# One-hot buffers handed over in two halves, x W1 inside the edge counting, and degrees from a column of ones, in a four-layer graph network on one NeuronCore

## The chip, the cores and the metric

The kernel runs on one core of a Trainium2 chip. The metric is device time in microseconds (us) of one execution, 5030.59 in the median of three runs. The engines are TensorE (PE in the profile, its weight loads PEld), VectorE (DVE), ScalarE (ACT), GpSimd (POOL) and SyncE (SP), which issues the DMAs. Each runs its own instructions in order; they meet at semaphores.

## The reference, cut to what matters

A graph has 1250 nodes with 512 features, and 20000 edges `src -> dst`, sorted by `dst`, each with a weight. Four blocks follow each other, each with a residual and a layer norm. Only the first is touched:

```python
deg  = segment_sum(ones, dst, 1250) + 1.0
inv  = rsqrt(deg)
def gcn_conv(x, W, b):                     # twice, relu after each
    h   = x @ W
    agg = segment_sum(h[src] * (inv[src] * inv[dst])[:, None], dst, 1250)
    return agg + h * (inv * inv)[:, None] + b
h = relu(gcn_conv(relu(gcn_conv(x, W1, b1)), W2, b2))
h = gru(h, W_ih, W_hh, b_ih, b_hh)         # 1250 steps one after the other
x = layernorm(x + h @ W_fc + b_fc)
```

The other blocks are a two-sided convolution with batch norm, a mixture of four experts over mean aggregation, and an aggregation by the edge weights. They use the edge count matrix, 1 / max(degree, 1) and the edge weight matrix that the first part of the kernel makes.

## The kernel before, in words

Nodes are cut into NT = 10 tiles of NP = 125. `adj_v` is the 1250 x 1250 matrix of edge counts (source on partitions and tiles, destination on columns), `wt_v` that of summed weights. Aggregation is a matrix product with `adj_v`.

*Counting.* The 160 groups of EP = 125 edges form 80 pairs (halves h = 0, 1), and the destinations 25 windows of WD = 50 columns. For each window DVE goes over the pairs that touch it. For each half it builds two one-hot matrices: `src_hot` (125 edges x 1250 sources, padded to HOT = 1254; before.py line 879) and `dst_hot` (125 x 4 x 50, with a one and the three parts of the edge weight, line 880). There is one buffer for each half. PE (`window`, lines 396 to 414) multiplies them: for each of the ten source tiles three small matmuls (line 411), 30 for each half, summed in two PSUM banks. `hot_ready0/1` hands a buffer to PE, `hot_used0/1` gives it back after the 30 matmuls. Matmuls with a matrix of zeros open and close a window (lines 403 and 414), and ACT (`take_window`, line 685) copies it out, with two sets of banks in turn. PE, DVE and ACT loop over windows; PE reads two registers from `bounds` at each window's start, and DVE two with some arithmetic.

*Between counting and conv1.* SP writes the counts (line 218) and the weights (line 220) to DRAM. PE sums the count matrix over the sources with a matrix of ones, 30 matmuls (line 426), the in-degree in a row on all partitions. DVE adds one (line 893), takes the maximum with one (line 894); PE turns the degrees into columns (line 435); GpSimd takes the power -0.5 (line 301); PE spreads the root over all partitions (line 443) between tiles of h1 = x W1 (`rows_product`, line 353), which ACT copies to `hn` (line 668). DVE adds the self loops on the diagonal (line 909) once the counts are out, and scales `adj_v` by the root of source and destination (line 910).

*conv1 and after.* `agg_cols` (line 363) makes 12 column blocks of 417 by ten matmuls each in four banks; ACT adds the bias with relu (line 660) into `r2`. PE turns `adj_v` block by block (line 458), and DVE copies the turned matrix to `wt_v` (line 919), which SP writes to DRAM for a later block. h2 and conv2 go as h1 and conv1, beside DVE's work on the recurrent weights (lines 922 to 953). Then come the input products of the recurrent stage (line 476, read out on DVE at line 969) and its 1250 steps (line 495), from about 693 to 3896 us.

Of the kernel before, what the change touches and what calls it, by code (L numbers as in the profile page):

```python
# [26 lines left out]
ALU = mybir.AluOpType  # L27
# [7 lines left out]
P = 128  # L35
# [16 lines left out]
COPIES = 16  # L52


def layout(nc, io):

    ctx = ExitStack()
    with ctx:
# [62 lines left out]
        e_col = hn_f[:, 1250:1250 + 3 * ET].rearrange("p (a t) -> p a t", a=3)  # L121
        e_src, e_dst, e_w = e_col[:, 0], e_col[:, 1], e_col[:, 2]
        w_part = hn_f[:, 1730:2370].rearrange("p (t a) -> p t a", a=4)
# [10 lines left out]


# [66 lines left out]
        def _(sp):  # L202
# [48 lines left out]
            sp.wait_ge(s("cnt_out0"), 16)  # L251
# [32 lines left out]
        def _(pool):  # L284

            pool.memset(ident[:], 0.0).then_inc(s("ident0"), 1)
# [4 lines left out]
            pool.wait_ge(s("ident0"), 1)  # L291
# [45 lines left out]
        def _(pe):  # L337
# [39 lines left out]
            pe.wait_ge(s("const"), 9)  # L377
# [17 lines left out]
            pe.wait_ge(s("plan"), 4)  # L395
            def window(w, u):
# [23 lines left out]
            for w in range(NW // 2 * 2, NW):  # L420
# [7 lines left out]
            pe.wait_ge(s("xcols_in"), 16)  # L428
            pe.wait_ge(s("w1_in"), 16)

            pe.wait_ge(s("win_read"), NW + 2)

            pe.wait_ge(s("deg1"), 3)
            for t in range(NT):
                m = mm(psum[0:NP, 7, t:t + 1], inv_row[0:1, t * NP:(t + 1) * NP], ones[0:1, 0:1], start=True, stop=True, skip_group_check=True)
            m.then_inc(s("deg1_turn"), 1)

            def inv_everywhere(h1_tile):

                if h1_tile == 2:  # L440
                    pe.wait_ge(s("inv_col_ready"), 1)
                    for t in range(NT):
                        m = mm(psum[:, 4 + t // 4, (t % 4) * NP:(t % 4 + 1) * NP], inv_col[0:NP, t:t + 1].to_broadcast([NP, P]), ident[0:NP, 0:NP],
                               start=True, stop=True, skip_group_check=True)
# [839 lines left out]
```

## Time and profile before

| What | us |
|---|---|
| median of three runs | 5030.59 (5028.41 to 5030.91) |
| the profiled execution | 5028.03 |
| its span, first to last instruction | 5025.8 |
| TensorE busy | 4893.7 (97%) |
| TensorE weight loads busy | 4218.9 (84%) |
| DVE busy | 2881.4 (57%) |
| ACT busy | 1950.6 (39%) |
| mean granted TensorE clock, share of full speed | 0.988 |

The profile is one execution. Busy time is counted for each engine; matmuls are pipelined, so their busy times overlap and a mean is longer than the distance from one to the next. "Idle before" is the time in which the engine did nothing ahead of an instruction, with what ended it; "issue" there means that nothing in the profile ended it. fp32 matmuls stand as two records each. A merged row of the timeline gives the start of the first and the time to the end of the last of its instructions.

### The profile page before, as it was taken

Reading aid. Unit: us, or ns where it says so; the run is one execution under the profiler, and the core shown is the slowest. Engines: PE = TensorE matmul, PEld = TensorE weight load, DVE = VectorE, ACT = ScalarE, POOL = GpSimd, SP = SyncE. Lnnn points to the kernel's source line nnn. Section 1 sums busy time; section 2 is a strip of 40 time slices with the busy share of each in tenths; the row PEclk is TensorE's granted clock in tenths of the full one; section 3 lists DMA queues with packets and bytes.
Section 4 is the critical chain, followed back from the end, with each engine's and each line's share of the span. In section 5 each row is a group of like instructions: output and inputs, shape, how many; then the busy total and the mean of one; then the engine's idle time right before and its main releaser. Section 6 shows DMA issues by size and latency. Waiting matters only on the chain.

```text
span 5025.8 us, 335766 instructions
## 1 busy us (share of the span) xinstructions
PE 4893.7 (97%) x131794; PEld 4218.9 (84%) x131795; DVE 2881.4 (57%) x16350; ACT 1950.6 (39%) x15372; POOL 841.4 (17%) x5071
## 2 busy tenths in 40 slices
PE   7889999999999999999999999999999999999989
PEld 7765569999999999999999999999999445555554
DVE  6551346666666666666666666666666625445551
ACT  0110025555555555555555555555555001122110
POOL 0000002222222222222222222222222000000000
PEclk9999999999999999999999999999999999999989
DMA  1011210000000000000000000000000100011011
GB/s 62 0 67 67 99 49 0 0 0 0 0 0 0 0 0 0 0 0 0 0 0 0 0 0 0 0 0 0 0 0 0 60 17 20 18 36 37 25 50 41
DMA packets 28932, 81.11 MB, mean 16 GB/s; under 512 B 1594, under 2 KB 1834, under 8 KB 28858
## 3 DMA queue, kind: packets, MB, share of 16 engines
q1 hardware_dynamic: 28858, 80.03, 4.3%
q8 instruction: 57, 0.93, 0.1%
q14 instruction: 17, 0.14, 0.0%
HBM read 58.08 MB, written 21.95 MB: 16 GB/s over the span
## 4 chain that ended last, share of the span: by engine, by line
PE 94%; DVE 2%; issue 2%; DVEq 1%; ACT 0%; POOL 0%; DMA 0%; ACTq 0%; SPq 0%; POOLq 0%
PE psum L495 63%; PE psum L567 8%; PE psum L363 5%; PE psum L353 4%; PE psum L579 4%; PE psum L411 3%; PE psum L476 2%; PE psum L553 2%; PE psum L643 2%; DVE r L880 1%; PE psum L426 0%; PE psum L458 0%; DVEq L875 0%; DVE r L879 0%; DVE stat L813 0%
## 5 line engine op out<-in xcount | busy, mean ns | idle before, releaser
L495 PE MATMUL psum<-h,r 128*128 128x16 f16 (+1 forms) x80000 | 3008.5, 181 | 9.6 <-ACT psum L707 4.5
L495 PEld LDWEIGHTS psum<-h,r 128*128 128x128 f16 x80000 | 2639.5, 96 | 11.0 <-DVEq L993 5.2
L495 PE MATMUL psum<-h,hn 128*128 128x16 f16 (+1 forms) x40000 | 2124.3, 177 | 0.0
L495 PEld LDWEIGHTS psum<-h,hn 128*128 128x128 f16 x40000 | 1591.5, 96 | 0.0
L999 DVE TENSOR_TENSOR_SCAN psum<-mul_rz,psum 128x6 f32<-128x6 f32 x5000 | 854.3, 171 | 536.7 <-PE psum L495 488.1
L707 ACT COPY psum<-big 128x2 f32 (+1 forms) x7506 | 1003.3, 163 | 0.0
L315 POOL TENSOR_TENSOR upd_add<-upd,signs 128x4 f32<-128x4 f32 x2500 | 499.3, 200 | 2542.0 <-DVE upd L1018 1779.2
L720 ACT ACTIVATE mul_n<-psum 128x2 f32<-128x2 f32 x2500 | 433.7, 173 | 1123.2 <-DVE psum L999 1123.1
L1018 DVE TENSOR_TENSOR_SCAN upd<-upd_mul,upd_add 128x8 f32<-128x8 f32 x2500 | 418.1, 167 | 300.4 <-ACT upd_mul L725 300.4
L729 ACT ACTIVATE upd_add<-psum 128x2 f32<-128x2 f32 x2500 | 433.1, 173 | 297.5 <-DVE psum L1005 297.5
L1014 DVE TENSOR_TENSOR_SCAN h<-upd_mul,upd_add 128x8 f16<-128x8 f32 x2500 | 425.8, 170 | 169.2 <-POOL upd_add L315 4.4
L1028 DVE TENSOR_TENSOR h<-upd,h 128x2 f16<-128x2 f32 x2500 | 421.7, 169 | 86.1
L316 POOL COPY r<-upd 128x2 f32 x2500 | 468.5, 187 | 0.0
L1005 DVE TENSOR_TENSOR_SCAN psum<-mul_n,psum 128x8 f32<-128x8 f32 x2500 | 446.6, 179 | 33.6
L725 ACT ACTIVATE upd_mul<-psum 128x2 f32<-128x2 f32 x2500 | 433.2, 173 | 49.5
L411 PE MATMUL psum<-r 125*128 125x50 bf16 (+1 forms) x6240 | 240.2, 197 | 15.4 <-DVE r L880 11.2
L363 PE MATMUL psum<-adj,hn 125*128 125x417 f32 (+1 forms) x720 | 252.7, 512 | 2.1 <-ACT hn L668 1.4
L411 PEld LDWEIGHTS psum<-r 125*128 125x128 bf16 x6240 | 226.5, 100 | 28.6 <-DVE r L880 24.1
L363 PEld LDWEIGHTS psum<-adj,hn 125*128 125x128 f32 x720 | 135.7, 189 | 119.6 <-issue 115.0
L567 PE MATMUL psum<-adj,r 128*125 128x512 f16 x960 | 217.3, 383 | 8.3 <-DVE r L1210 8.3
L567 PEld LDWEIGHTS psum<-adj,r 128*125 128x125 f16 x960 | 132.0, 138 | 87.6 <-issue 13.1
L353 PE MATMUL psum<-ws,r 128*125 128x512 f32 x400 | 180.2, 613 | 7.2 <-ACT r L747 5.9
(224 smaller groups left out, 2532.7 us busy)
## 6 DMA issues: line engine op xcount, KB each, us to landing
ws<-in_Wl SPq DMA_DIRECT2D x9, 1024.0 KB, 5.4
ws<-in_Wr SPq DMA_DIRECT2D x9, 1024.0 KB, 7.6
edge_counts<-adj SPq DMA_DIRECT2D x2, 3051.8 KB
edge_weights<-big SPq DMA_DIRECT2D x1, 6103.5 KB
adj_rows<-big SPq DMA_DIRECT2D x1, 6103.5 KB
adj<-adj_rows SPq DMA_DIRECT2D x1, 6103.5 KB
big<-edge_counts SPq DMA_DIRECT2D x1, 6103.5 KB
adj<-edge_weights SPq DMA_DIRECT2D x1, 6103.5 KB
```

Of the source, the lines that this page charges most:

```text
L315: pool.tensor_tensor(start[:, :, 1:3], new[:, :, 2:3].broadcast_to([P, 2, 2]), signs[:].rearrange("p (j a) -> p j a", a=2), ALU.mult).then ...
L316: pool.tensor_copy(r1[:, 2 * c:2 * c + 2, bass.ds(t, 1)], upd[:, 1 - u, c, 2:8:4]).then_inc(s(f"gru_kept{c}"), 1)
L363: m = mm(o[:, 0:n1 - n0], rows[0:NP, t, f * P:(f + 1) * P], mat[0:NP, t, n0:n1], start=(t == 0), stop=(t == NT - 1))
L411: m = mm(to, src_hot[0:EP, h, t * NP:t * NP + P], dst_hot[0:EP, h, columns], start=False, stop=False, skip_group_check=True)
L495: m = mm(places, whh16[g][:, part, 2 * kc + k, (2 * c + j) * P:(2 * c + j + 1) * P], state.unsqueeze(1).broadcast_to([P, COPIES, 2 - part] ...
L567: m = mm(o, a(pa), b(pb), start=start and i == 0, stop=stop and i == 2)
L707: return nc.scalar.copy(columns, big[:, bass.ds(t * 12 + c * 6 + 2 * g, 2)])
L720: nc.scalar.activation(mul_n[:, c, 3:8:4], sum_rz[c][0][:, 2:6:3], ACT.Sigmoid).then_inc(s(f"gru_r{c}"), 1)
L725: nc.scalar.activation(upd_mul[:, c, 2:8:4], sum_rz[c][1][:, 2:6:3], ACT.Sigmoid).then_inc(s(f"gru_z{c}"), 1)
L729: nc.scalar.activation(upd_add[:, c, 0:8:4], sum_n[c][:, 3:8:4], ACT.Tanh).then_inc(s(f"gru_n{c}"), 1)
L999: v.tensor_tensor_scan(sum_rz[c][g], mul_rz[:], psum[:, 4 * c + g, 0:6], 0.0, ALU.mult, ALU.add).then_inc(s(f"gru_{'rz'[g]}_sum{c}"), 1)
L1005: v.tensor_tensor_scan(sum_n[c], mul_n[:, c], psum[:, 4 * c + 2, 0:8], 0.0, ALU.mult, ALU.add).then_inc(s(f"gru_n_sum{c}"), 1)
```

## The change

It has these parts:

- `src_hot` is built and given back in two parts of 625 columns: DVE builds columns 0 to 624 after `hot_part` (PE done with tiles 0 to 4), then `dst_hot` after `hot_used` (all ten), and signals `hot_first`; then columns 625 to 1249, and signals `hot_ready`. PE waits for `hot_first` ahead of tile 0 and for `hot_ready` ahead of tile 4, which reads up to column 627.
- A column of ones at 1250 of `src_hot` makes row 125 of the last tile of `adj_v` the in-degree. The 30 matmuls of line 426 go; ten turns of one column give degree columns, and everything else comes from these. Both 1/degree and the root are spread over the partitions by ten matmuls each, before conv1.
- h1 = x W1 is made inside the counting loop in bank 4: half a tile (two of four products) ahead of each of windows 0 to 23, the operand staged and the result copied by ACT. Twelve rounds for ten tiles; two tiles are made twice.
- The counts are written out in five transfers of 250 columns, as windows are done, in place of two at the end.
- `adj_v` is no longer scaled. The rows of h are scaled on ACT, the columns of the result on DVE (`scale_cols`), then ACT adds the bias with relu in place (`shift_cols`). The turned matrix is scaled on DVE as it is copied. The edge columns and weights move from `hn` to `big`, and the addition of the output bias to x moves behind counting's end.

The core of the diff, with `...` where lines are left out:

```diff
+H1 = NW // 2
...
+        x_stage = big[:, tail + 7 * ET:tail + 7 * ET + KT * NP].rearrange("p (k n) -> p k n", k=KT)
...
-            sp.wait_ge(s("win_counts"), NW)
-            for h in range(2):
-                half = slice(5 * h, 5 * h + 5)
-                sp.dma_start(tiles(d_cnt[half]), adj_v[0:NP, half]).then_inc(s(f"cnt_out{h}"), 16)
+            for q in range(NW // 5):
+                sp.wait_ge(s("win_counts"), 5 * q + 5)
+                columns = slice(5 * q * WD, (5 * q + 5) * WD)
+                sp.dma_start(tiles(d_cnt)[:, :, columns], adj_v[0:NP, :, columns]).then_inc(s(f"cnt_out{5 * q // (NW - 5)}"), 16)
...
+            pool.memset(src_hot[:, :, N:N + 1], 1.0).then_inc(s("const"), 1)
+            pool.memset(src_hot[:, :, N + 1:HOT], 0.0).then_inc(s("const"), 1)
...
-            def agg_cols(name, bank0, rows, mat):
+            def agg_cols(name, bank0, rows, mat, read="stored", first=None):
...
-                        o = out_rows(i, bank0, None, f"{name}_stored")
+                        o = out_rows(i, bank0, None, f"{name}_{read}")
                         for t in range(NT):
+                            if first and i == 0:
+                                first(t)
...
+            def h1_half(i, u):
+
+                if u == 0:
+                    pe.wait_ge(s("x_staged"), i + 1)
+                    pe.wait_ge(s("h1_stored"), i + 1)
+                for k in range(2 * u, 2 * u + 2):
+                    m = mm(psum[0:NP, 4], x_stage[:, k], wslot(0)[:, k], start=(k == 0), stop=(k == KT - 1), skip_group_check=True)
+                if u == 1:
+                    m.then_inc(s("h1_done"), 1)
...
                     for h in range(2):
-                        pe.wait_ge(s(f"hot_ready{h}"), g + 1)
                         for t in range(NT):
+                            if t == 0:
+                                pe.wait_ge(s(f"hot_first{h}"), g + 1)
+                            if t == 4:
+                                pe.wait_ge(s(f"hot_ready{h}"), g + 1)
...
+                            if t == 4:
+                                m.then_inc(s(f"hot_part{h}"), 1)
                         m.then_inc(s(f"hot_used{h}"), 1)
...
-            with pe.Fori(0, NW // 2) as i:
+            pe.wait_ge(s("w1_in"), 16)
+            with pe.Fori(0, H1) as i:
                 for u in range(2):
+                    h1_half(i, u)
                     window(2 * i + u, u)
...
             pe.wait_ge(s("win_counts"), NW)
-            for c, (n0, n1) in enumerate(NCH):
+            for t in range(NT):
+                m = mm(psum[0:NP, 7, t:t + 1], adj_v[:, NT - 1, t * NP:(t + 1) * NP], ident[:, NP:NP + 1], start=True, stop=True, skip_group_check=True)
+            m.then_inc(s("plan_turned"), 1)
+            pe.wait_ge(s("win_read"), NW + 2)
+            pe.wait_ge(s("h1_stored"), H1 + 1)
+            for b, (name, column) in enumerate((("invdeg_col_ready", invdeg_col), ("inv_col_ready", inv_col))):
+                pe.wait_ge(s(name), 1)
                 for t in range(NT):
-                    m = mm(psum[:, 4 + c, 0:n1 - n0], ones[0:NP], adj_v[0:NP, t, n0:n1], start=(t == 0), stop=(t == NT - 1))
-                m.then_inc(s("deg"), 1)
...
-            rows_product("h1", 0, r1, wslot(0), before=inv_everywhere)
-            pe.wait_ge(s("h1_stored"), NT)
-            pe.wait_ge(s("norm"), NT)
-            agg_cols("conv1", 4, hn, adj_v)
...
+            pe.wait_ge(s("invdeg_ready"), 1)
+            agg_cols("conv1", 4, hn, adj_v, "scaled", first=lambda t: (pe.wait_ge(s("h1_scaled"), t + 1), pe.wait_ge(s("loops"), t + 1)))
...
+            with act.Fori(0, H1) as i:
+                take_window(2 * i, 0)
+                act.wait_ge(s("h1_done"), i + 1)
+                nc.scalar.copy(hn[0:NP, bass.ds(i * NT // H1, 1)].rearrange("p t n -> p (t n)"), psum[0:NP, 4]).then_inc(s("h1_stored"), 1)
+                stage((i + 1) % H1)
+                take_window(2 * i + 1, 1)
...
+            for t in range(NT):
+                nc.scalar.activation(hn[0:NP, t], hn[0:NP, t], ACT.Copy, scale=inv_col[0:NP, t:t + 1]).then_inc(s("h1_scaled"), 1)
...
+                        dve.wait_ge(s(f"hot_part{h}"), offset + pair + 1)
+                        v.tensor_scalar(src_hot[0:EP, h, 0:N // 2], iota16[0:EP, 0:N // 2], e_src[0:EP, bass.ds(column, 1)], None, ALU.is_equal)
                         dve.wait_ge(s(f"hot_used{h}"), offset + pair + 1)
-                        v.tensor_scalar(src_hot[0:EP, h], iota16[0:EP], e_src[0:EP, bass.ds(column, 1)], None, ALU.is_equal)
...
-                            op0=ALU.is_equal, op1=ALU.mult).then_inc(s(f"hot_ready{h}"), 1)
...
+                            op0=ALU.is_equal, op1=ALU.mult).then_inc(s(f"hot_first{h}"), 1)
+                        v.tensor_scalar(src_hot[0:EP, h, N // 2:N], iota16[0:EP, N // 2:N], e_src[0:EP, bass.ds(column, 1)], None, ALU.is_equal).then_inc(s(f"hot_ready{h}"), 1)
...
+            def add_loops(t0, t1):
...
+            dve.wait_ge(s("cnt_out0"), 64)
+            add_loops(0, NT - 2)
+            for b, row_of in enumerate((invdeg_row, inv_row)):
+                dve.wait_ge(s("inv_rows"), b + 1)
+                for c in range(3):
+                    n0, n1 = 4 * NP * c, min(4 * NP * (c + 1), N)
+                    link(v.tensor_copy(row_of[:, n0:n1], psum[:, 4 - 4 * b + c, 0:n1 - n0]))
+                dve.sem_inc(s(("invdeg_ready", "inv_rows_read")[b]), 1)
+            dve.wait_ge(s("cnt_out1"), 16)
+            add_loops(NT - 2, NT)
...
+            scale_cols("conv1", 4, r2, 0, 12)
...
-                    v.tensor_copy(wt_v[0:NP, d, 4 * q * NP:4 * q * NP + width], psum[0:NP, n % 4, 0:width]).then_inc(s("tr_stored"), 1)
...
+                    v.scalar_tensor_tensor(out=wt_v[0:NP, d, 4 * q * NP:4 * q * NP + width], in0=psum[0:NP, n % 4, 0:width], scalar=inv_col[0:NP, d:d + 1],
+                                           in1=inv_row[0:NP, 4 * q * NP:4 * q * NP + width], op0=ALU.mult, op1=ALU.mult).then_inc(s("tr_stored"), 1)
```

## Rows read from the trace of the kernel before

**Rows 1.** The page, busy times: us, share of the span, instructions.

```profile
PE 4893.7 (97%) x131794; PEld 4218.9 (84%) x131795; DVE 2881.4 (57%) x16350; ACT 1950.6 (39%) x15372; POOL 841.4 (17%) x5071
```

**Rows 2.** Grouped lines of the counting stage: busy, mean ns, idle before, releaser.

```profile
L411 PEld LDWEIGHTS psum<-r 125*128 125x128 bf16 x6240 | 226.5, 100 | 28.6 <-DVE r L880 24.1
```

**Rows 3.** Timeline, a steady pair: start, duration, what, idle before, releaser.

```profile
27.99 2.06 PEld L411 LDWEIGHTS psum<-r 125*128 125x128 bf16 x60 [0.28 <-DVE r L880]
...
29.41 0.55 DVE L879 TENSOR_SCALAR r<-r,hn 125x1254 bf16<-125x1254 f16 x1 [0.44 <-PE psum L411]
29.87 0.42 DVE L880 SCALAR_TENSOR_TENSOR r<-r,hn 125x200 bf16 x1
30.34 2.06 PEld L411 LDWEIGHTS psum<-r 125*128 125x128 bf16 x60 [0.29 <-DVE r L880]
```

**Rows 4.** Timeline, two runs of 180 matmuls, and a window boundary.

```profile
198.31 7.83 PE L411 MATMUL psum<-r 125*128 125x100 bf16 x180
...
207.76 6.82 PE L411 MATMUL psum<-r 125*128 125x100 bf16 x180 [0.25 <-DVE r L880]
...
303.61 0.19 PE L414 MATMUL psum<-r 125*128 125x1 bf16 x2
...
304.44 0.55 DVE L879 TENSOR_SCALAR r<-r,hn 125x1254 bf16<-125x1254 f16 x1 [1.88 <-issue]
...
305.24 0.54 DVE L879 TENSOR_SCALAR r<-r,hn 125x1254 bf16<-125x1254 f16 x1
...
305.38 4.46 PE L411 MATMUL psum<-r 125*128 125x100 bf16 x120 [0.32 <-DVE r L880]
```

**Rows 5.** Busy times by stretch; then granted clock, DMA share, GB/s.

```profile
180.00:240.00 60.00, 49.80 (x1230) 46.72 (x1228) 34.92 (x81) 6.33 (x12) 0.00 (x0) 0.90 0.00 0
```

**Rows 6.** Timeline of PE, from the last counting matmuls to conv1.

```profile
309.69 0.19 PE L414 MATMUL psum<-r 125*128 125x1 bf16 x2
310.56 21.25 PE L426 MATMUL psum<-adj,ones 125*128 125x417 f32 x60 [0.68 <-ACT adj L685]
332.66 2.31 PE L435 MATMUL psum<-ones,big 1*125 1x1 f32 x20 [0.85 <-DVE big L893]
334.90 8.83 PE L353 MATMUL psum<-ws,r 128*125 128x512 f32 x16
343.56 2.39 PE L443 MATMUL psum<-ident,inv_col 125*128 125x125 f32 x20
345.79 27.63 PE L353 MATMUL psum<-ws,r 128*125 128x512 f32 x64
374.10 1.32 PE L363 MATMUL psum<-adj,hn 125*128 125x417 f32 x3 [0.68 <-ACT hn L668]
```

**Rows 7.** Timeline, the short instructions of the same stretch.

```profile
335.08 0.17 DVE L896 TENSOR_SCALAR invdeg_col<-psum 125x10 f32<-125x10 f32 x1 [2.07 <-PE psum L435]
...
335.54 1.98 POOL L301 TENSOR_TENSOR inv_col<-inv_col,minus_half 125x10 f32<-125x10 f32 x1 [331.76 <-DVE inv_col L897]
...
346.00 1.84 DVE L904 COPY big<-psum 128x500 f32<-128x500 f32 x3 [2.42 <-PE psum L443]
...
361.60 0.29 DVE L909 TENSOR_TENSOR adj<-adj,ident 125x125 f32<-125x125 f32 x1 [4.85 <-DMA edge_counts<-adj]
```

**Rows 8.** DMA by stretch (last: share, GB/s): the opening, the copy-out.

```profile
6.00:8.00 2.00, 1.00 1.00 410
...
320.00:340.00 20.00, 19.15 (x62) 10.49 (x61) 7.07 (x7) 0.00 (x0) 1.98 (x1) 0.91 0.32 128
```

**Rows 9.** Grouped lines, 4300 to 4500 us: a scaling group on DVE.

```profile
L1228 DVE SCALAR_TENSOR_TENSOR adj<-psum,esc,adj 125x512 f32<-125x512 f32 x10 | 7.5, 751 | 25.4 <-ACT adj L794 25.1 <-DVE top L1121 0.2
```

**Rows 10.** Timeline, the transposes on PE and their copies on DVE.

```profile
458.16 14.47 PE L458 MATMUL psum<-ident,adj 125*125 125x125 f32 x100
...
458.86 15.05 DVE L919 COPY big<-psum 125x500 f32<-125x500 f32 x30 [88.39 <-PE psum L458]
```

**Rows 11.** The page, grouped lines of the whole span.

```profile
L567 PE MATMUL psum<-adj,r 128*125 128x512 f16 x960 | 217.3, 383 | 8.3 <-DVE r L1210 8.3
```

More of the change, by code:

```diff
@@ L428, in _ @@
[L428 to L444, printed above, removed]
-                    m.then_inc(s("inv_rows"), 1)
@@ new lines, in _ @@
+            for b, (name, column) in enumerate((("invdeg_col_ready", invdeg_col), ("inv_col_ready", inv_col))):
+                pe.wait_ge(s(name), 1)
+                for t in range(NT):
+                    m = mm(psum[:, 4 - 4 * b + t // 4, (t % 4) * NP:(t % 4 + 1) * NP], column[0:NP, t:t + 1].to_broadcast([NP, P]), ident[0:NP, 0:NP],
+                           start=True, stop=True, skip_group_check=True)
+                m.then_inc(s("inv_rows"), 1)
+            pe.wait_ge(s("invdeg_ready"), 1)
@@ L465, in _ @@
             pe.wait_ge(s("tr_stored"), 3 * NT)
-            agg_cols("conv2", 0, hn, adj_v)
+            agg_cols("conv2", 0, hn, adj_v, "scaled")
             pe.wait_ge(s("conv2_stored"), 12)
@@ L662, in take_cols, with take_rows, shift_cols @@
                         i += 1
-            def take_rows(name, bank0, base=0):
+            def take_rows(name, bank0, base=0, scale=None):
                 for t in range(NT):
                     act.wait_ge(s(f"{name}_done"), base + t + 1)
-                    nc.scalar.copy(hn[0:NP, t], psum[0:NP, bank0 + t % 4]).then_inc(s(f"{name}_stored"), 1)
+                    if scale is None:
+                        m = nc.scalar.copy(hn[0:NP, t], psum[0:NP, bank0 + t % 4])
+                    else:
+                        m = nc.scalar.activation(hn[0:NP, t], psum[0:NP, bank0 + t % 4], ACT.Copy, scale=scale[0:NP, t:t + 1])
+                    m.then_inc(s(f"{name}_stored"), 1)
+            def shift_cols(name, dst, bias):
+                i = 0
+                for f in range(KT):
+                    for n0, n1 in NCH:
+                        act.wait_ge(s(f"{name}_scaled"), i + 1)
+                        nc.scalar.activation(dst[:, f, n0:n1], dst[:, f, n0:n1], ACT.Relu, bias=bias[:, f:f + 1]).then_inc(s(f"{name}_stored"), 1)
+                        i += 1
             def take_turned(name, bank0, to=r2):
@@ L687, in take_window, with stage @@
                 act.sem_inc(s("win_read"), 1)
-            with act.Fori(0, NW // 2) as i:
-                for u in range(2):
-                    take_window(2 * i + u, u)
-            for w in range(NW // 2 * 2, NW):
+            def stage(i):
+                nc.scalar.copy(x_stage, r1[:, :, bass.ds(i * NT // H1 * NP, NP)]).then_inc(s("x_staged"), 1)
+            act.wait_ge(s("xcols_in"), 16)
+            stage(0)
+            with act.Fori(0, H1) as i:
[4 more added lines that the diff above has]
+                take_window(2 * i + 1, 1)
+            for w in range(2 * H1, NW):
                 take_window(w, w % 2)
-            take_rows("h1", 0)
+            act.wait_ge(s("h1_stored"), H1 + 1)
+            act.wait_ge(s("inv_col_ready"), 1)
+            for t in range(NT):
+                nc.scalar.activation(hn[0:NP, t], hn[0:NP, t], ACT.Copy, scale=inv_col[0:NP, t:t + 1]).then_inc(s("h1_scaled"), 1)
             act.wait_ge(s("small_in"), 48)
-            act.wait_ge(s("fc_bias_used"), 1)
-            take_cols("conv1", 4, r2, ACT.Relu, b1c)
-            take_rows("h2", 4)
-            take_cols("conv2", 0, r1, ACT.Relu, b2c)
+            shift_cols("conv1", r2, b1c)
+            take_rows("h2", 4, scale=inv_col)
+            shift_cols("conv2", r1, b2c)
             act.wait_ge(s("gru_init"), 1)
-            nc.scalar.activation(warm[:], scl[:, 1:2], ACT.Sigmoid).then_inc(s("warm"), 1)
+            nc.scalar.activation(warm[:], scl[:, 1:2], ACT.Sigmoid)
             def put(t, c, g):
@@ L888, in _, with scale_cols @@
             link(v.tensor_tensor(xr[0:NP], xr[0:NP], fc_bias[0:NP].unsqueeze(1).broadcast_to([NP, NT, D]), ALU.add))
[L889 to L911 removed]
+            def scale_cols(name, bank0, dst, i0, i1):
+                for i in range(i0, i1):
+                    n0, n1 = NCH[i % 3]
+                    dve.wait_ge(s(f"{name}_done"), i + 1)
+                    v.tensor_tensor(dst[:, i // 3, n0:n1], psum[:, bank0 + i % 4, 0:n1 - n0], inv_row[:, n0:n1], ALU.mult).then_inc(s(f"{name}_scaled"), 1)
+            scale_cols("conv1", 4, r2, 0, 12)
             dve.wait_ge(s("wt_out"), 16)
@@ L928, in _ @@
             dve.sem_inc(s("top_part"), 1)
+            scale_cols("conv2", 0, r1, 4, 6)
             dve.wait_ge(s("top_all"), 1)
@@ L953, in _ @@
                 split(g, ws[:, 0:WSLOT])
-            dve.wait_ge(s("conv2_done"), 12)
+                scale_cols("conv2", 0, r1, 6 + 2 * g, 8 + 2 * g)
+            scale_cols("conv2", 0, r1, 10, 12)
             split(2, ws[:, WSLOT:2 * WSLOT])
```

67 lines of the change are left out of this document (29 added, 38 removed).

## The prediction

> **What bounds the kernel now.** I read the busy shares first [rows 1]. The reader is to see that TensorE is busy for 97% of the span: time goes away only where TensorE's own work, its half-rate clock or its gaps do. The recurrent stage after 660 us, most of the span, is not touched, so the sum is made in the counting stage and in what lies between it and the recurrent stage.
>
> Next come the grouped lines of the counting stage [rows 2]. 6240 weight loads are 104 pairs of edge groups of 60 matmuls each, spread over 25 windows of 50 columns. The timeline of one steady pair [rows 3] shows that a pair starts 2.35 us after the one before (27.99, 30.34) while its loads take 2.06 us. The idle 0.28 us is ended by DVE: the buffer of half 0 is given back when TensorE has done all its 30 matmuls, DVE starts building at 29.41, starts the second instruction at 29.87 and is done at 30.29, and TensorE starts at 30.34. So one buffer's round trip (1.04 us of reading, 0.38 until DVE starts, 0.88 of building, 0.05 to TensorE) sets 2.35, and not the work of either engine.
>
> The window boundary [rows 4]: after the last small matmul (303.61 + 0.19 = 303.80) TensorE reads two registers and waits, and the next window's first matmul starts at 305.38, 1.58 us later. DVE, coming from its own register arithmetic, starts at 304.44. Where the boundary was longer, a run of 180 matmuls took 7.83 us instead of 6.82 [rows 4], and the mean granted clock of 180 to 240 us is 0.90 [rows 5]: part of it ran at the lower level (1.2 GHz) after the idle time. By such pairs of rows I count nine windows with about 1.0 us of this each, some 9 us, beside the first window.
>
> Then the chain between counting and the first aggregation [rows 6]: last counting matmul ends at 309.88, the aggregation starts at 374.10, 64.2 us. It holds 21.25 us of degree matmuls, a 2.31 us turn, 40 products with W1 (8.83 + 27.63 us) and 2.39 us of spreading.
>
> **The change, part by part.** *Degrees.* The 30 wide matmuls go. A column of ones in the source buffer (column 1250; the last tile reads 128 columns from 1125) counts edges in row 125 of the last tile, inside matmuls already paid for: nothing added on TensorE. Afterwards, from the last counting matmul T: ACT's copy and hand-over 0.68 (the gap in the row of 310.56), ten turns of one column 2.31, DVE waits and runs three [125, 10] instructions at about 0.2 each (0.17 in [rows 7], plus links) to T+3.9. Spreading 1/deg takes 2.39 to T+6.3; spreading the root another 2.39 to T+8.7. GpSimd's power, 1.98 [rows 7], runs from T+3.5 to T+5.5, beside the first. DVE adds eight diagonals at 0.29 by T+6.2, then three copies of 1.84 together [rows 7], ready at T+8.3: just hidden; if slower, they are late next. So conv1 can start at T+8.8. The products at 334.90 took 8.83 for eight where 32 took 27.63, 1.9 us more, after small matmuls with waits between; I charge 2.0 for the same at conv1's start.
>
> *Copying the counts out.* The last of the five transfers is issued at T+0.7: 1.25 MB, 1250 runs of 1000 bytes. Before, such 125-partition copies moved at 128 GB/s with 0.32 of the DMA share [rows 8], which gives 9.8 us, and landing about T+13. If a run of 1000 bytes costs what a 2048- or 5000-byte run of the start costs, it is at most twice that: the opening transfers of both lengths go at 410 GB/s with all engines [rows 8], so length down to 2048 costs nothing, and 2048-byte prices give 20 us, T+23. conv1 needs tile 8 at T+8.8+8x0.70=T+14.4. Stall 0 to 8 us; I take 0.5, nearest to the rate rows. Four earlier transfers lie beside counting, 40 us before it ends. That the edge weights now queue behind 1.25 and not 6.25 MB only brings them forward.
> Sum of the chain: 64.2 becomes 8.8+2.0+0.5=11.3, **-52.9 us**. The row scaling of `adj` and 1250-wide reciprocals leave DVE; they lay beside the W1 products, so they give nothing by themselves.
>
> *W1 inside counting.* 24 half steps of two products at 27.63/32=0.86 [rows 6], 1.73 us, stand ahead of windows 0 to 23. Behind them DVE starts at the old point. Two registers are read beside the products if TensorE's sequencer runs ahead; then the first counting matmul starts at 1.73+0.15+0.3=2.2 us after the last one, against a mean of 1.67 (1.58, and 0.2 more at every second boundary). 24x0.5 = **+12**. Bounds: 0.2 each (5 us), or the register reads in series, 1.15 more each (+40). Window 0's step lies in the 2 us in which TensorE now waits for DVE (W1 has landed: with what is queued ahead of it 3.9 MB, at the 410 GB/s of [rows 8] 9.4 us after a start at 2 to 4, while the plan is ready at 14.8). The filled gaps should hold the clock at 2.4 GHz: **-9** (bounds 0, -11). ACT's copy and staging, 0.6 us each, fall into the middle of a window of 6 us or more, behind a finished window copy; the next one is not due, so no cost.
>
> *Two-part buffers.* Columns 0 to 624 are given back after tile 4, the rest after tile 9. DVE refills the first half early, so after the last release only the 0.42 us destination part [rows 3] remains: round trip 1.04+0.38+0.42+0.05=1.9, below TensorE's 2.06. Next in line is DVE: 0.80 us now for both instructions (304.44 to 305.24 [rows 4]); the third adds at least 0.17 (a small instruction [rows 7]) and at most 0.46 (the full one again): 0.97 to 1.26 a half, 1.94 to 2.5 a pair. Half the columns at the rate of the full row gives about 0.13 of fixed time, hence 1.9. TensorE gets two more waits and one more signal per half. So 2.06 to 2.35, and I take 2.15 for four extra semaphore steps: 79 pairs that are not a window's last times (2.35-2.15) is 16, less 1 for the last pairs: **-15**. The second half's build (0.3) lies behind tiles 0 to 3 (0.41 us).
> Counting: +12-9-15 = **-12**.
>
> *Later.* conv1 and conv2 scale on DVE and shift on ACT: one step more at conv2's end, +0.6 (a 417-column read of PSUM, from 0.75 for 512 [rows 9]); at conv1's end the transposes hide it. These transposes take 14.47 against 15.05 on DVE [rows 10], now with a scaling instruction of 0.75 instead of 0.61 [rows 7, 9]: 0 to +2.3, I take +1.5. Between conv2's columns DVE has maxima and splits, but only four banks must be ahead, 28 us. Scaling h rows rides on ACT copies that exist; scaling h1 rows (0.6 each against 0.70 of TensorE) stays ahead of the tiles. GpSimd's two small memsets end before DVE's cast that TensorE waits for.
>
> Sum: -52.9-12+0.6+1.5=-62.8. The profiled execution took 5028.0 (span 5025.8), 2.6 below the median 5030.6; so 4965 for it and **4968** as median.
>
> **Where the Trainium skill bears.** The build of 1254 columns is followed after 0.46 us [rows 3], far less than its columns at the 1.19 ns of one-wide instructions. The Trainium skill, "VectorE: DVE Perf Modes", Mode 2x_1P, asks for 4-byte alignment of 16-bit operands; the second part starts at column 625, off such a boundary. By that rule it falls behind, the slower rival below. Another page of the Trainium skill, "Vector Engine (DVE) Microarchitecture Reference", 5.1, says that alignment makes no difference; no row before shows an odd start.
> For the register reads: the branch on a loaded register in the middle of each group of L567 leaves 8.3 us of idle in 960 matmuls, all of it ended by DVE [rows 11], so control work was covered by queued matmuls. The Trainium skill, "Advanced Engine Details and Errata", Sequencer Loop, says other instructions are queued while control ones execute; by it the +12 stands, without it +40.
>
> **Rivals.**
> (a) The split gives nothing: DVE's third instruction takes the wait's place and a pair stays at 2.35. For it: DVE may need 1.26 a half. Against: fewer columns. +15: 4983. Chance 0.15.
> (b) The register reads don't overlap: +28: 4996. For it: before, each boundary shows 1.1 us of "issue" idle; against: [rows 11]. 0.08.
> (c) The last count transfer is late (runs priced as 2048 bytes): +8: 4976. 0.12.
> (d) Slower. The odd half loses its rate: one-wide instructions take 0.29 us for 125 columns and 0.75 for 512 [rows 7, 9], 1.19 ns a column, so 625 take 0.88, and 0.80 from start to start. If both parts fall, as odd counts, DVE needs 0.80+0.34+0.80=1.94 a half, 3.9 a pair: 104x3.9=406 where the pairs now take 79x2.35+25x2.2=241, +165, and with -53 and +5 of the rest 5148. It decides at 2.8 us a pair, 1.4 a half. If only the second part falls it is 1.43: about no change. Against: the build of 1254, no multiple of four either, keeps its 0.46. Chance 0.05 (slower 0.04, even 0.01).
> The forecast, 4955 to 4977, holds 0.50 and the better cases beside it (pair at 2.07, step at 1.9: 4945 to 4955) 0.10; that the degrees or W1 did not leave the chain I hold impossible.
> Range 4948 to 4991, which holds (a) and (c) and leaves out (b), (d) and the lowest. 0.2% is 10 us, about what a measurement tells from no change. Faster 0.95, same 0.01, slower 0.04.
>
> **What would show it.** A pair period of 2.1 to 2.2 us with no gap ended by DVE; a boundary of about 2.2 us filled by products; granted clock near 1 from 60 to 300 us; T near 298; conv1 starting 11 us after T; one landing wait at tile 8 at most. A DVE build of the half above 0.46 us, a pair above 2.35, or idle of over 1 us after each W1 step would prove it wrong.

## The result, and the profile after

| What | before | after |
|---|---|---|
| median, us | 5030.75 (5028.41 to 5036.87, four runs) | 4938.18 (4937.91 to 4947.04, four runs) |
| ratio | | 0.9818, 95% interval 0.9801 to 0.9835 |
| span of the profiled execution, us | 5025.8 | 4936.1 |
| granted TensorE clock, mean | 0.988 | 0.992 |

The kernel became 92.6 us faster, more than forecast: 4938 lies below the range of 4948 to 4991. Three of its four executions took 4938 us and one took 4947.04; experiment 8 comes back to such steps of 9 us. The page of the kernel after, busy times (us, share of the span, instructions), answers to [rows 1]:

```profile
PE 4848.5 (98%) x131770; PEld 4189.5 (85%) x131771; DVE 2896.4 (59%) x16568; ACT 1965.2 (40%) x15397; POOL 841.9 (17%) x5073
```

TensorE still bounds the kernel. Its busy time fell by 45 us where the span fell by 90: the other half was idle time. (Time at half rate counts as busy.) Read from the timelines of the two profiled executions, stage by stage:

| Stage | before | after | difference | forecast |
|---|---|---|---|---|
| first counting matmul starts at | 18.53 | 19.24 | +0.7 | 0 |
| inside the 25 windows (104 pairs) | 251.34 | 215.63 | -35.7 | -15 pairs, -9 clock |
| the 24 boundaries | 40.01 | 44.90 | +4.9 | +12 |
| last counting matmul (T) to conv1 | 64.22 | 9.92 | -54.3 | -52.9 |
| conv1 to the first recurrent step | 323.97 | 326.24 | +2.3 | +2.1 |
| recurrent stage, 1250 steps | 3198.1 | 3194.3 | -3.8 | 0 |
| all later stages | 1129.7 | 1125.9 | -3.8 | 0 |
| sum | | | -89.7 | -62.8 |

**Inside a window.** The grouped lines of the counting stage after (busy, mean ns, idle before, releaser), first the window's weight loads, then those of the W1 products; compare [rows 2]:

```profile
L431 PEld LDWEIGHTS psum<-r 125*128 125x128 bf16 x6240 | 206.3, 97 | 7.2 <-DVE r L921 6.8
L409 PEld LDWEIGHTS psum<-ws,big 128*125 128x125 f32 x93 | 15.7, 188 | 13.4 <-issue 12.6
```

The idle time that DVE ended fell from 24.1 to 6.8 us. The timeline of a steady stretch, DVE and TensorE's loads, answers to [rows 3]; a row gives start, duration, what:

```profile
44.60 3.07 PEld L431 LDWEIGHTS psum<-r 125*128 125x128 bf16 x93 [0.17 <-DVE r L921]
44.76 0.38 DVE L919 TENSOR_SCALAR r<-r,big 125x625 bf16<-125x625 f16 x1
45.05 0.42 DVE L921 SCALAR_TENSOR_TENSOR r<-r,big 125x200 bf16 x1
45.39 0.38 DVE L926 TENSOR_SCALAR r<-r,big 125x625 bf16<-125x625 f16 x1
45.68 0.38 DVE L919 TENSOR_SCALAR r<-r,big 125x625 bf16<-125x625 f16 x1
```

93 loads follow each other without a gap, 33 ns each, and DVE, catching up here, starts a half 0.92 us after the one before (44.76, 45.68) where TensorE needs 1.03 [rows 3]. TensorE's own work is the bound now. A window of seven pairs took 14.48 us, 2.07 a pair.

**The boundary.** TensorE, two boundaries after; compare the third of [rows 4]:

```profile
186.71 0.19 PE L436 MATMUL psum<-r 125*128 125x1 bf16 x2
186.76 1.96 PE L409 MATMUL psum<-ws,big 128*125 128x512 f32 x4
188.56 0.19 PE L420 MATMUL psum<-r 125*128 125x1 bf16 x2
188.62 6.21 PE L431 MATMUL psum<-r 125*128 125x100 bf16 x180
194.67 0.19 PE L436 MATMUL psum<-r 125*128 125x1 bf16 x2
194.99 1.52 PE L409 MATMUL psum<-ws,big 128*125 128x512 f32 x3
```

From the end of the closing matmuls (186.90) to the first of the next window (188.62) it is 1.72 us, and the two products (four records) fill nearly all of it. The register reads and the opening matmuls are out of sight behind them. Every second boundary takes 2.00, since there the products start 0.13 us after the end of the closing ones (194.99 against 194.86) and not 0.14 before it. The run of 180 matmuls takes 6.21 us here, and no run of 180 takes more than 6.3. The granted clock says the same; the stretch of [rows 5] after (busy times, clock, DMA share, GB/s):

```profile
180.00:240.00 60.00, 59.28 (x1400) 50.23 (x1399) 45.06 (x136) 11.78 (x22) 0.00 (x0) 1.00 0.07 21
```

**The chain from counting to conv1.** TensorE's timeline after; compare [rows 6]:

```profile
279.58 0.19 PE L436 MATMUL psum<-r 125*128 125x1 bf16 x2
280.45 2.34 PE L449 MATMUL psum<-ident,adj 128*125 128x1 f32 x20 [0.68 <-ACT adj L711]
283.53 4.09 PE L456 MATMUL psum<-ident,invdeg_col 125*128 125x125 f32 x20 [0.74 <-DVEq L932]
287.46 2.40 PE L456 MATMUL psum<-ident,inv_col 125*128 125x125 f32 x20
289.69 1.59 PE L370 MATMUL psum<-adj,hn 125*128 125x417 f32 x4
```

The first ten spreading matmuls took 4.09 us and not 2.39; the 2.0 us of slow start that the forecast laid on conv1 came here, and conv1 starts at its full rate. It is a stretch at half rate. The granted clock (the 0.50 below) says so of these matmuls, and of the slow W1 products from which the forecast took the 2.0, here first the kernel after, then the kernel before (TensorE alone, then clock, DMA share, GB/s):

```profile
283.70:287.10 3.40, 3.40 (x17) 0.50 0.34 105
336.00:339.40 3.40, 3.40 (x6) 0.50 0.32 128
```

Beside it, DVE and the queue of the last count transfer:

```profile
283.48 1.68 DVE L938 TENSOR_TENSOR adj<-adj,ident 125x125 f32<-125x125 f32 x8 [0.15 <-DVE invdeg_col L931]
287.66 1.85 DVE L946 COPY big<-psum 128x500 f32<-128x500 f32 x3 [2.50 <-PE psum L456]
289.89 1.84 DVE L946 COPY big<-psum 128x500 f32<-128x500 f32 x3 [0.39 <-PE psum L456]
294.15 0.49 DVE L938 TENSOR_TENSOR adj<-adj,ident 125x125 f32<-125x125 f32 x2 [2.42 <-DMA edge_counts<-adj]
```

```profile
280.42 0.25 SPq L221 DMA_DIRECT2D edge_counts<-adj  x1
```

The transfer of the last 250 columns had landed 13.7 us after its issue (forecast 12.3). Its tile 8 is added by 294.4, and conv1 asks for it at about 289.69 + 8 x 0.70 = 295.3: in time, by 0.9 us only.

**The transposes**, with the scaling in DVE's copy, answer to [rows 10]:

```profile
373.68 16.05 PE L470 MATMUL psum<-ident,adj 125*125 125x125 f32 x100
```

+1.6 us, against a forecast of +1.5. DVE's 20 wide ones took 730 ns each.

### The profile page after: what moved, and what is told of

It is laid out like the page before. It is cut to its first block, busy times and chain, and to the rows that moved or that the text cites. A ratio compares the mean times of both kernels' runs of the same rounds, so it can differ in the third digit from the quotient of the medians.

```text
span 4936.1 us, 336038 instructions
## 1 busy us (share of the span) xinstructions
PE 4848.5 (98%) x131770; PEld 4189.5 (85%) x131771; DVE 2896.4 (59%) x16568; ACT 1965.2 (40%) x15397; POOL 841.9 (17%) x5073
## 4 chain that ended last, share of the span: by engine, by line
PE 92%; DVE 4%; issue 2%; DVEq 1%; ACT 0%; POOL 0%; POOLq 0%; ACTq 0%
PE psum L507 65%; PE psum L579 8%; PE psum L370 5%; PE psum L591 4%; PE psum L358 4%; PE psum L488 2%; PE psum L565 2%; PE psum L655 2%; DVE r L926 1%; DVE r L921 1%; DVE r L919 1%; PE psum L431 0%; PE psum L470 0%; DVEq L921 0%; DVEq L913 0%
## 5 line engine op out<-in xcount | busy, mean ns | idle before, releaser
L431 PE MATMUL psum<-r 125*128 125x50 bf16 (+1 forms) x6240 | 212.6, 192 | 2.9 <-DVE r L921 0.5
L431 PEld LDWEIGHTS psum<-r 125*128 125x128 bf16 x6240 | 206.3, 97 | 7.2 <-DVE r L921 6.8
L591 PE MATMUL psum<-hn,big 125*125 125x512 f16 x800 | 179.3, 379 | 0.0
```

## The experiments

All are the kernel after with one edit, but the second. A count of time "in the windows" goes from a window's first matmul to its closing ones, summed over 25. T is the end of the last counting matmul, and "the chain" is the time from T to conv1's start. Each total is a median; the kernel before had 5025 to 5030 beside them.

**1. The split undone** (`e1_no_split`): one hand-over for each buffer, all else as in the kernel after. DVE's side of the edit, shortened:

```diff
-    dve.wait_ge(s(f"hot_part{h}"), offset + pair + 1)
-    v.tensor_scalar(src_hot[0:EP, h, 0:N // 2], iota16[0:EP, 0:N // 2], ...)
     dve.wait_ge(s(f"hot_used{h}"), offset + pair + 1)
+    v.tensor_scalar(src_hot[0:EP, h, 0:N], iota16[0:EP, 0:N], ...)
...
-    ....then_inc(s(f"hot_first{h}"), 1)
-    v.tensor_scalar(src_hot[0:EP, h, N // 2:N], iota16[0:EP, N // 2:N], ...).then_inc(s(f"hot_ready{h}"), 1)
+    ....then_inc(s(f"hot_ready{h}"), 1)
```

> The changed kernel with the two-part hand-over undone: one build of 1250 columns after hot_used, one signal. Theory (the buffer's round trip set the pair, and the products with W1 in the boundaries keep the clock up): the pair goes back to 2.35 us, 79 pairs x 0.3 = +24 us, the granted clock stays at 1.00 in the counting stage, time 4938 + 24 = 4962. Rival (the clock's half-rate stretches came from the waits inside the pairs): they come back as well, +12 more, 4974. Rival (the third DVE instruction had cost what the split gave): no more than 4948.

Measured: 4970.53 (ratio to before 0.9878, 0.9862 to 0.9895). In the windows 240.47 us, 24.8 more than with the split; boundaries 44.45; T at 303.54; the chain 9.92 as before the edit. The loads' group, to be laid beside that of the kernel after:

```profile
L429 PEld LDWEIGHTS psum<-r 125*128 125x128 bf16 x6240 | 214.7, 97 | 23.3 <-DVE r L914 19.1
```

The wait on DVE is back. Counting accounts for 23.8 of the 34.4 us by which this profiled span (4970.5) is longer; 10.9 lie in stages after the recurrent one that the edit doesn't touch (see experiment 8). The half-rate stretches did not come back: the granted clock from 19 to 300 us is 1.00, so the first rival is wrong although the total lies near its 4974.

**2. The split alone** (`e2_split_only`): the kernel before, and only the two-part build and hand-over (with a memset for the columns past 1250, which the shorter builds no longer write).

> The kernel before with the two-part hand-over alone. Theory: pairs at 2.07 us, in-window time -24 us; the window boundaries are as idle as before, so the half-rate stretches stay (about 12 us of them): 5031 - 24 = 5007. Rival (a busier window is enough to hold the clock): another -12, 4995. Rival (the split pays only together with the products ahead of a window, which let DVE get ahead): under 10 us, above 5021.

Measured: 5006.56 (0.9957, 0.9940 to 0.9974). In the windows 222.26 (before 251.34), boundaries 39.70, T at 281.05, chain 65.85, later stages +7.2 against before. The total met the expected 5007 in part by luck: counting fell by 29.4 us and not 24, and the later stages made up for it. The trace, two boundaries and a window between them:

```profile
189.01 0.19 PE L420 MATMUL psum<-r 125*128 125x1 bf16 x2
190.34 0.20 PE L404 MATMUL psum<-r 125*128 125x1 bf16 x2 [1.14 <-issue]
190.74 6.22 PE L415 MATMUL psum<-r 125*128 125x100 bf16 x180 [0.20 <-DVE r L889]
196.81 0.19 PE L420 MATMUL psum<-r 125*128 125x1 bf16 x2
198.56 0.20 PE L404 MATMUL psum<-r 125*128 125x1 bf16 x2 [1.56 <-ACTq L693]
```

The pair is 2.07 us with or without the products. What remains are four windows of four pairs that take 9.62 us where others take 8.3, and the idle boundaries. So of -35.7 us in the windows, -23.9 are the shorter pair (the sum without half-rate stretches went from 239.5 to 215.6), and the rest is clock. The split alone brings 5.2 of that rest.

**3. No W1 products** (`e3_no_w1_products`). h1 is left out; two small matmuls with zeros for each tile keep the signals, and ACT's staging and copies stay.

```diff
-    for k in range(2 * u, 2 * u + 2):
-        m = mm(psum[0:NP, 4], x_stage[:, k], wslot(0)[:, k], start=(k == 0), stop=(k == KT - 1), ...)
     if u == 1:
-        m.then_inc(s("h1_done"), 1)
+        mm(psum[0:NP, 4, 0:500], zero_b[0:NP, 0:NP], zero_b[0:NP, 0:500], start=True, stop=True, ...)
+        mm(psum[0:NP, 4, 500:512], zero_b[0:NP, 0:NP], zero_b[0:NP, 0:12], start=True, stop=True, ...).then_inc(s("h1_done"), 1)
```

> The changed kernel without the 48 products with W1 in the counting loop (h1 is left out; two small matmuls with zeros per tile keep the signals). Theory (the products fill a boundary that is idle anyway and hold the clock at 2.4 GHz): the boundary falls from 1.87 to about 1.6 us, -7, the half-rate stretches come back, +12: 4943, so 41 us of products cost nothing or less. Rival (products cost their time less the old idle): 24 x 0.37 = -9 without any clock effect, 4929. Rival (products cost their full 41 us): 4897.

Measured: 5050.51 (1.0040, 1.0025 to 1.0054), a surprise in two ways. First, counting got longer without its 41 us of products: T at 290.11, 10.3 us later than with them. The boundaries are 1.81 us each (with the products 1.87), and ten windows run partly at half rate, as in these two equal windows of 240 matmuls:

```profile
126.01 9.59 PE L430 MATMUL psum<-r 125*128 125x100 bf16 x240
...
147.48 8.16 PE L430 MATMUL psum<-r 125*128 125x100 bf16 x240
```

In the windows it is 227.39, 11.8 more. Second, the recurrent stage, hundreds of microseconds later, took 3285.9 and not 3194.3 us. The stretch from 1000 to 3000 us (TensorE, loads, DVE, ACT, POOL; clock, DMA share, GB/s):

```profile
1000.00:3000.00 2000.00, 2000.00 (x73198) 1957.52 (x73195) 1264.19 (x9148) 1053.22 (x9145) 495.24 (x3050) 1.00 0.00 0
```

At a clock of 1.00, TensorE's loads stand idle for 42.5 us, and 2100 fewer matmuls fit in. This edit removes instructions from TensorE's program ahead of that loop, which leads to the next two.

**4. The same, with TensorE's program filled up** (`e8_no_products_refilled`): experiment 3 and, after counting, three products with results that nobody reads. Experiment 3 had taken six matmul records net out of the loop; the three fp32 products put six back ahead of what follows.

```diff
     for w in range(2 * H1, NW):
         window(w, w % 2)
+    for u in range(3):
+        mm(psum[0:NP, 5], x_stage[:, u], wslot(0)[:, u], start=True, stop=True, skip_group_check=True)
```

> The kernel without the products with W1 in the counting loop (h1 left out), plus three unused products once, right after counting, so that TensorE's program behind them lies where it lay in the changed kernel. In the run without them the untouched recurrent stage took 3285.9 us against 3194.3, 92 us more, with a gap inside the loop that nothing ends. Theory (where the loop's instructions lie sets this): the stage returns to about 3194 and the time to 5050 - 92 + 3 = 4961, i.e. still 10 above the changed kernel's counting stage plus the 2.6 of the three products. Rival (the missing products or the missing values of h1 slow the recurrent stage): it stays at 3286, 5053.

**5. The three unused products alone** (`e9_three_more`): the same lines added to the kernel after.

> The changed kernel plus the same three unused products right after counting. Theory (position): their own time is 2.6 us; the later loops shift by as much again the other way, so the recurrent stage may move by anything between -4 and +92 us, while the counting stage stays (last counting matmul at 279.8). Rival (position does not matter): 4938 + 3 = 4941, recurrent stage 3194.

Measured: 4954.74 (0.9857, 0.9840 to 0.9873) and 4951.27 (0.9846, 0.9829 to 0.9862). The recurrent stage is 3194.6 and 3194.1 us, and the same stretch of experiment 4 reads:

```profile
1000.00:3000.00 2000.00, 2000.00 (x75300) 2000.00 (x75297) 1301.72 (x9413) 1083.05 (x9414) 506.47 (x3138) 1.00 0.00 0
```

So the 92 us of experiment 3 (2628.7 against 2555.5 ns a step) don't hang on the products: three more instructions ahead of the loop take them away. That it is the place of the loop's instructions in TensorE's program which does it is the likely reading, but argued: no run moved the loop alone. Moving it on by the same three from the kernel after changes nothing, nor do the 30 matmuls of experiment 8 or the four more unrolled windows of experiment 10 (3194.3, 3194.9), so only some places would be bad, and which ones stays open.

With that out of the way the products can be priced, but the price depends on what they are laid beside. Against experiment 4, T falls from 290.38 to 279.87, by 10.5 us. But experiment 4 keeps the small matmuls, staging and copies, and its boundaries are 1.83 us each where those of experiment 2, with nothing ahead of a window, are 1.65. Counting, as the sum of windows and boundaries in us:

| | one hand-over | two parts |
|---|---|---|
| W1 after counting | 291.35 (before) | 261.96 (experiment 2) |
| W1 in the boundaries | 284.92 (experiment 1) | 260.53 (after) |

By this table the products are worth -6.4 us without the split and -1.4 with it, where the forecast had +3, and the split is worth -29.4 without and -24.4 with them. Why experiment 4 runs more of its windows at half rate than experiment 2 was not tried.

**6. Register reads ahead of the products** (`e4_registers_first`): `h1_half(i, u)` is called inside `window`, after the two register reads and not before them.

```diff
     blocks = pe.value_load(bounds[0:1, 1, bass.ds(w, 1)], min_val=1, max_val=EH)
     before = pe.value_load(bounds[0:1, 2, bass.ds(w, 1)], min_val=0, max_val=EH * (NW + 1))
+    if i is not None:
+        h1_half(i, u)
```

> The changed kernel with the half step of W1 issued after the window's two register loads in place of ahead of them. Theory (TensorE's sequencer loads the registers while queued products run): now the loads lie bare after the old window, 1.1 us for each of 24 boundaries, +26 us: 4964, boundary about 2.9 us. Rival (the boundary is set by DVE, which starts at its own time, 1.5 us after the last matmul): 1.1 + 1.73 = 2.8 is still later than DVE, same 4964, but an idle gap ended by DVE would show. Rival (loads cost TensorE nothing): 4938.

Measured: 4978.80 (0.9903, 0.9886 to 0.9919); boundaries 76.85 in sum, 3.20 each in the mean; in the windows 215.24. One of the shorter boundaries:

```profile
205.18 0.19 PE L438 MATMUL psum<-r 125*128 125x1 bf16 x2
206.42 1.98 PE L409 MATMUL psum<-ws,big 128*125 128x512 f32 x4 [1.04 <-issue]
208.23 0.19 PE L422 MATMUL psum<-r 125*128 125x1 bf16 x2
208.28 3.89 PE L433 MATMUL psum<-r 125*128 125x100 bf16 x115
```

The 1.04 us of "issue" idle are the reads, with nothing queued on TensorE. The same instructions behind the products cost nothing that shows: 32 us for the order of two calls.

**7. All count transfers at the end** (`e6_copies_last`): each of the five waits for all windows.

```diff
-    sp.wait_ge(s("win_counts"), 5 * q + 5)
+    sp.wait_ge(s("win_counts"), NW)
```

> The changed kernel with all five transfers of the counts issued after the last window. Theory: the DVE adds the self loops only when four of them, 4.9 MB, have landed: at 128 GB/s 39 us, plus 2 of latency, then 1.7 + 1.85 us of DVE: conv1 starts about 46 us after the last counting matmul in place of 9.9, time 4938 + 36 = 4974. Rival (runs of 1000 bytes are paid as 2048 ones): twice that, 5012. TensorE's program is the same, so the recurrent stage stays at 3194.

Measured: 4996.24 (0.9936, 0.9916 to 0.9955). T at 279.48, and the chain grew from 9.92 to 54.06 us. The queue, DVE and TensorE:

```profile
280.13 43.38 SPq L221 DMA_DIRECT2D edge_counts<-adj  x5
```

```profile
329.99 1.68 DVE L938 TENSOR_TENSOR adj<-adj,ident 125x125 f32<-125x125 f32 x8 [46.95 <-DMA edge_counts<-adj]
...
342.18 0.49 DVE L938 TENSOR_TENSOR adj<-adj,ident 125x125 f32<-125x125 f32 x2 [6.75 <-DMA edge_counts<-adj]
```

```profile
333.54 8.55 PE L370 MATMUL psum<-adj,hn 125*128 125x417 f32 x16 [43.97 <-DVEq L947]
```

Four transfers of 1.25 MB took 49.9 us (280.13 to 329.99) and the fifth 12.2 more: 100 GB/s with the wait for landing, 104 in the trace between 281 and 330 us, at 0.34 of the DMA share, where the forecast's rate [rows 8] was 128. The price of the short runs lies between its two bounds, 9.8 and 20 us, near the lower. The Trainium skill, "DMA: Bandwidth & Descriptors", in "Why a DMA increments its semaphore by 16 and not by 1", says that a transfer uses the largest number of engines, up to 16, that divides the slowest dimension of both its sides. For 125 that gives five of 16, 0.31 as an estimate; the trace shows 0.34. The expected 4974 was missed by 22 us: 8 in the chain, 3.5 between conv1 and the recurrent stage, and 11 in the late stages that experiment 8 turns to.

**8. The wide degree matmuls put back** (`e7_wide_degrees`): 30 matmuls of 417 columns after counting, their result unread.

```diff
+    pe.wait_ge(s("h1_stored"), H1 + 1)
+    for c, (n0, n1) in enumerate(NCH):
+        for t in range(NT):
+            mm(psum[:, 4 + c, 0:n1 - n0], ones[0:NP], adj_v[0:NP, t, n0:n1], start=(t == 0), stop=(t == NT - 1))
```

> The changed kernel with the 30 wide degree matmuls of the old kernel put back between counting and the ten turns, their result unused. Theory (they stood bare on the path): their old time, 21.2 us, +21 in the chain: conv1 starts 31 us after the last counting matmul in place of 9.9. Rival (a transfer or GpSimd would have set conv1's start anyway and they hide beside it): under 5 us. The recurrent stage may shift by its position on top of this.

Measured: 4968.41 (0.9880, 0.9860 to 0.9900), the chain 30.84 us, +20.9 for:

```profile
280.60 21.25 PE L451 MATMUL psum<-adj,ones 125*128 125x417 f32 x60 [0.68 <-ACT adj L715]
```

Its total is 30 above the kernel after, and the other 9 us are again in late stages. Over the twelve profiled executions of this study the expert stage (from the first load of expert weights to that of the last layer's) took 754.9, 755.0, 758.2, 758.3, 758.5 (before), 760.8 and, six times, 762.8 to 763.0 us. Experiments 7 and 9, which leave TensorE's program as it is, are among the six, and the kernel after had 755.0. The time goes with the clock: from the end of the recurrent stage the granted clock is 0.97 in the kernel after and 0.96 in experiments 1, 7 and 9. So this is a spread of some 8 us between executions, and totals nearer to each other than that tell nothing of one edit; the counting times repeat within 1 us and can. The kernel after has it too: its fourth execution, 4947.04, had a mean clock of 0.989 where the other three had 0.991 to 0.992. So some 9 of the 92.6 us are not safe.

**9. An even split** (`e5_even_split`): the second part starts at column 624.

> The kernel after with the build of the source buffer split at column 624 instead of 625, so that the second part starts at an even column; the part that is handed over still ends at tile 4. (Columns 625 and on are read by tiles 5 to 9; column 624 is then written with the second part, so the first hand-over's waits are unchanged and tile 4 also waits for the second part by the same semaphore as before.) My theory: TensorE's 2.06 us per pair is the bound and the odd start costs nothing, so counting (first to last counting matmul), the pair of 2.07 us and the total are those of the kernel after (215.6 us in the windows, T at 279.8, total 4938 within 0.3%). Rival: the odd start halves the rate of the second part, which an even start would give back: the second part's 0.38 us would fall to about 0.2 us, and window ends and boundaries would be shorter by some 2 us in all.

Measured: 4947.69 (0.9844, 0.9828 to 0.9861), T at 279.32, in the windows 215.18. The group of the second part, first here, then in the kernel after:

```profile
L926 DVE TENSOR_SCALAR r<-r,big 125x626 bf16<-125x626 f16 x208 | 79.3, 381 | 0.0
```

```profile
L926 DVE TENSOR_SCALAR r<-r,big 125x625 bf16<-125x625 f16 x208 | 78.3, 377 | 0.0
```

An odd start costs nothing. The total's 9 us above the kernel after are the expert stage's 763.0 again.

**10. Ten tiles in ten rounds** (`e10_ten_tiles`): no tile is made twice, and the last five windows have no products ahead of them.

```diff
-H1 = NW // 2
+H1 = NT
```

> The kernel after with H1 = NT: the W1 products of the ten tiles lie ahead of the first 20 windows (one tile in two windows, no tile done twice), and the last five windows, unrolled, have no products ahead of them. Theory 1 (the products are free inside the boundaries, by the run that left them all out and was 10.3 us longer in counting): the four removed products ahead of windows 20 to 23 give nothing or cost up to 2 us of half-rate clock; T 278 to 282; chain 9.9; the total within 0.3% of the kernel after except for the recurrent stage, which can differ since 200 instructions more stand ahead of it on TensorE's queue. Theory 2 (each product costs its 0.86 us of TensorE): four steps of 1.73 us less, T near 273 and the total 6.9 us less.

Measured: 4947.42 (0.9844, 0.9827 to 0.9860). The boundaries fell by 1.4 us to 43.53; one window of two pairs took 5.50 and not 4.08 us, at half rate again; T 279.15, and the chain 11.14. Four products less gave 0.6 us at T and lost 1.2 behind it, where 6.9 would be their price. No variant that ran beat the kernel after, though this one and experiment 9 are too near to it to be told apart by their totals.

## Why the prediction was wrong

The mechanisms were as forecast in the main; several sizes were not, and each large miss had the same sign. The forecast sum of -62.8 is 26.9 short of the -89.7 of the profiled executions: 8.9 in the pair, 7.1 in the boundary, 2.8 in the clock, 1.4 in the chain, and 7.6 in untouched stages, less 0.9 in the rest. By terms:

- **The pair, -15 forecast, -23.9 measured.** The step that failed: "So 2.06 to 2.35, and I take 2.15 for four extra semaphore steps". The steps cost nothing; the pair is 2.07 at TensorE's own 2.06. DVE was charged with 0.97 to 1.26 a half and needs 0.92: its instructions follow each other after 0.29, 0.34 and 0.29 us. The saving also counts at window ends, which the 79 pairs left out.
- **The boundary, 2.2 us forecast, 1.87 measured: +4.9 and not +12.** The second step that failed: "the first counting matmul starts at 1.73+0.15+0.3=2.2 us after the last one". The products were added to 0.15 and 0.3 us of opening work; these lie behind them as well. And products stand in 23 of the 24 boundaries, since window 0's lie ahead of counting; the last boundary takes 1.53. The answer to rival (b) was right, and experiment 6 shows what it would have cost: +32, near the +28 priced.
- **The clock, -9 forecast, -11.8 measured.** Half-rate stretches were in ten windows, the first among them, which the count left aside. The forecast laid all of it on the filled gaps. Filled gaps do give it without the split (in experiment 1 the windows take 240.47 us, 0.9 above their sum at full rate), but the split alone gives 5.2 too. Together, products and clock are a gain of 1.4 us beside the split, where the forecast had +12 - 9 = +3.
- **The chain, -52.9 forecast, -54.3 measured.** Right to 1.4 us: the 0.5 of stall didn't occur, and the slow start, a half-rate stretch, came at the spreading matmuls.
- **conv2's end and the transposes**, +2.1 forecast, +2.3 measured: right. Counting starts 0.7 us later, which wasn't forecast; it comes with the split (19.09 with it alone, 18.62 in experiment 1, 18.53 before).
- **Stages that the change doesn't touch were charged 0** and came out 7.6 us shorter. The later ones' 3.8 are inside their spread. The recurrent stage's 3.8 are not spread: eight edits of the kernel after (all but experiment 3) give 3194.0 to 3194.9, the split alone 3197.1, before 3198.1. Experiments 3 and 4 show that edits ahead of the loop can do such things; whether that is so here was not tried by itself and stays open.

T came at 279.8 and not near 298. The rivals: (a) a pair that stays at 2.35, (b) register reads in series, (c) a late last transfer and (d) a lost rate in the odd half are all excluded by the trace after and by experiments 1, 6, 7 and 9. The last transfer was in time with 0.9 us to spare, so (c) was the closest. The rule that speaks against an odd start, the 4-byte alignment of the Trainium skill, "VectorE: DVE Perf Modes", Mode 2x_1P, doesn't hold for this instruction: 377 ns at column 625, 381 at column 624. The rule of the Trainium skill, "Advanced Engine Details and Errata", Sequencer Loop, that other instructions can be queued while control ones execute, agrees with experiment 6 as far as that goes: matmuls queued ahead of the register reads run beside them, and with nothing queued the reads cost 1.04 us.

The lowest case, with a pair at 2.07 and a boundary at 1.9, stood in the prediction with a chance of 0.10. Its price (4945 to 4955) still misses by 7 us, nearly the stages charged 0. With the fourth execution's late stages, 4947, the forecast range would have been missed by 1 us and not 10, so how far it missed is in part luck; the terms above are not. Both values were TensorE's own work without any added overhead, readable in [rows 3] and [rows 6]; a margin was put on each instead, one on top of the other.

## What to carry to other kernels

When a buffer's round trip sets the pace and a split takes it below the engine's own work, forecast the engine's own work: a semaphore wait that is already met cost nothing here. Independent work put into gaps that hold control instructions can be free or a little better where the gaps also cost clock, but only if it stands ahead of the control instructions in the engine's order. Price such work against a kernel without it, not against one with stand-ins: here the two gave 1.4 and 10.5 us. After an edit ahead of a long loop, look at the loop's time per step too, even where the edit can't reach it.

## What the runs showed of the hardware that was not expected

- A loop of TensorE with the same instructions ran at 2628.7 ns a step, and at 2555.7 once three matmuls were added ahead of it: 92 us over 1250 steps, at a granted clock of 1.00 in both. The cause is open.
- 48 fp32 products of 512 columns (0.86 us each) ahead of 24 windows cost counting nothing: it was 1.4 us shorter than with the split alone, 6.4 us shorter without the split, and 10.5 us shorter than with small stand-ins.
- DVE's one-wide build of 625 columns is followed after 0.29 us, at an odd start too; 1254 columns were followed after 0.46 [rows 3].
- Runs of 1000 bytes from 125 partitions went to DRAM at 100 GB/s, 12.5 us for 1250 of them.
